# Top-k attention: a weight picked by a mark instead of a second exp; self-attention: six score banks throughout, and whole rounds of one kind

## The reference

```python
def _topk_cross_attn(h, ctx, w_q, b_q, w_kv, b_kv, w_co, b_co):
    q = (h @ w_q + b_q).reshape(B, L, H, D)
    kv = (ctx @ w_kv + b_kv).reshape(B, Lc, 2, H, D)
    scores = jnp.einsum('bqhd,bkhd->bhqk', q, k) / jnp.sqrt(jnp.float32(D))
    top_s, top_i = jax.lax.top_k(scores, TOPK)          # TOPK = 16
    attn = jax.nn.softmax(top_s, axis=-1)
    o = jnp.einsum('bhqk,bhqkd->bqhd', attn, vg).reshape(B, L, C)
    return o @ w_co + b_co

def mha(x, ctx, ...):                                   # third attention: ctx = x
    scores = jnp.einsum('bqhd,bkhd->bhqk', q, k) / np.sqrt(HD)
    attn = jax.nn.softmax(scores.astype(jnp.float32), axis=-1)
    out = jnp.einsum('bhqk,bkhd->bqhd', attn, v).reshape(Bq, Nq, D)
    return out @ wo + bo
```

## Time and profile before

| what | value |
|---|---|
| median of 3 runs | 1722.9 us (1711.07 to 1726.58) |
| the profiled execution | 1712.03 us, of which the span is 1710.2 us |
| busy: PE, DVE, ACT, POOL | 86%, 54%, 45%, 15% of the span |
| first attention | up to about 211 us |
| second attention (L919 first and last) | about 210 to 648 us |
| third attention (L857 and L895) | about 650 to 1401 us |
| fourth attention and the last MLP | to the end |

### The profile page before, as it was taken

One profiled execution on the slowest core, in us unless ns is written; L12 is line 12 of the kernel. 1 busy time (PEld: TensorE's weight loads), 2 busy tenths in 40 slices (PEclk: granted clock), 3 DMA queues, 4 the chain that ended last, 5 costly groups with the idle time before them and its releaser, 6 DMA issues.

```text
span 1710.2 us, 25890 instructions
## 1 busy us (share of the span) xinstructions
PE 1475.9 (86%) x9132; PEld 749.7 (44%) x9132; DVE 915.8 (54%) x2815; ACT 768.8 (45%) x1626; POOL 258.0 (15%) x504
## 2 busy tenths in 40 slices
PE   5999857788877787998898889998889789998998
PEld 3567534454644543353243333332323135453665
DVE  2555467766878785644445556665556225451111
ACT  2254445656666561224434445554445553334221
POOL 0020053443443532000000010000100001010110
PEclk9899967679898896999999989999999998999999
DMA  5022100000000001000010000000000000000000
GB/s 168 1 81 77 48 1 13 7 1 2 4 1 2 26 1 33 1 1 1 1 62 1 0 1 1 1 1 1 1 11 1 1 2 2 11 2 4 13 16 25
DMA packets 22096, 26.78 MB, mean 16 GB/s; under 512 B 4204, under 2 KB 19634, under 8 KB 21708
## 3 DMA queue, kind: packets, MB, share of 16 engines
q1 hardware_dynamic: 21059, 25.03, 4.6%
q10 hardware_dynamic: 909, 0.10, 0.0%
HBM read 21.58 MB, written 3.08 MB: 14 GB/s over the span
## 4 chain that ended last, share of the span: by engine, by line
PE 73%; ACT 9%; DVE 8%; issue 6%; POOL 3%; DMA 0%; ACTq 0%; SPq 0%; POOLq 0%; DVEq 0%
PE bank L857 27%; PE bank L814 9%; PE bank L895 7%; PE bank L829 6%; PE bank L793 5%; PE bank L772 3%; PE bank L919 3%; ACT pr L1081 2%; ACT exp_all L1098 2%; PE bank L751 2%; DVE part_max L1294 1%; ACT h_t L1023 1%; POOL probs L1402 1%; ACT left L1104 1%; PE bank L933 1%
## 5 line engine op out<-in xcount | busy, mean ns | idle before, releaser
L1081 ACT ACTIVATE pr<-bank 128x512 f32<-128x512 f32 x656 | 355.8, 596 | 458.6 <-PE bank L857 458.1
L1294 DVE TENSOR_REDUCE part_max<-bank 128x1 f32<-128x512 f32 x512 | 328.8, 685 | 283.6 <-PE bank L857 282.6
L857 PE MATMUL bank<-slot 32*128 32x512 f32 (+1 forms) x3072 | 430.8, 532 | 18.8 <-ACT pr L1081 14.1
L857 PEld LDWEIGHTS bank<-slot 32*128 32x128 f32 x3072 | 173.8, 188 | 243.4 <-issue 161.0
L1344 POOL TENSOR_SCALAR var_eps<-mean_var 128x4 f32<-128x4 f32 x24 | 5.5, 227 | 1103.9 <-DVE mean_var L1258 1103.7
L895 PE MATMUL bank<-pr,v 128*17 128x512 f32 x1024 | 138.6, 614 | 14.3 <-ACT pr L1081 14.3
L814 PE MATMUL bank<-h_t,w_m 128*128 128x512 f32 x256 | 133.2, 646 | 6.4 <-ACT h_t L1023 4.4
L1098 ACT ACTIVATE exp_all<-bank,neg 128x154 f32<-128x154 f32 x256 | 86.2, 395 | 57.8 <-POOL neg L1389 57.1
L1319 DVE MAX8 top<-bank 128x8 f32<-128x154 f32 x256 | 69.4, 312 | 65.7 <-PE bank L919 64.4
L919 PE MATMUL bank<-kc,slot 32*128 32x154 f32 x512 | 59.9, 357 | 45.1 <-ACT exp_all L1098 44.9
L1104 ACT ACTIVATE left<-left,neg 128x154 f32<-128x154 f32 x256 | 95.4, 434 | 0.0
(11 more groups left out here) (141 smaller groups left out, 1927.6 us busy)
## 6 DMA issues: line engine op xcount, KB each, us to landing
w_m<-in_L_xcond_w_m SPq DMA_DIRECT2D x1, 2048.0 KB, 8.6
w_m<-in_L_xcond_w_m SPq DMA_DIRECT2D x2, 1024.0 KB, 6.8
w<-in_L_xcond_w SPq DMA_DIRECT2D x2, 1024.0 KB, 6.6
w_ada<-in_L_xcond_w_ada SPq DMA_DIRECT2D x1, 1792.0 KB, 10.3
x_sb<-in_x SPq DMA_DIRECT2D x6, 256.0 KB, 6.6
res_row<-rows_dram SPq DMA_DIRECT2D x12, 128.0 KB, 3.4
out_x<-x_sb SPq DMA_DIRECT2D x6, 256.0 KB, 2.1
wa<-in_L_xcond_w_qkv SPq DMA_DIRECT2D x1, 768.0 KB, 7.3
```

Source lines behind the costliest of these rows:

```text
L857: last = nc.tensor.matmul(g.bank(*tile)[:, into], left, right, start=True, stop=True)
L1081: nc.scalar.activation(m.pr[:, u % NPR, :], g.bank("s", gi, i)[:, :], ACT.Exp).then_inc(g.free("s", gi, i), 1)
L1294: nc.vector.tensor_reduce(m.part_max[:, slot, h * TB + i // 8, i // 4 % 2:i // 4 % 2 + 1], bank[:, :], axis=AX.X, op=ALU.max).then_inc(don ...
```

## The change

In the second attention `c_exp_left` is gone. In place of `c_diff` stands `c_pick` on POOL: it first turns `left2` into marks (1 where the value is exactly -1e30, else 0; one operation on 128x308), waits for that, and multiplies the marks with `exp_all`, in the same two pieces. It waits for `left2` of DVE and `c_exp_all` of ACT. `c_neg` now waits for an older `c_exp_all` instead of an older `c_exp_left`. The planned places of the steps around it move too: the turn, the copy and the product with the values come earlier, and the scores of the next token tile a little later, behind the turn and the copy.

In the third attention, scores use banks 1 to 6 for all groups, and the ring banks 0 to 2 for all. Where a round would be of one kind (m alone at the start, s alone at the end), it holds four tiles, every second time; this holds for the first attention too.

```diff
     if kind in ("m", "m_turn", "s"):
-        return (1, 2, 3, 4, 5, 6) if 20 <= step[1] < 24 else (3, 4, 5, 6)
+        return (1, 2, 3, 4, 5, 6) if attention(step[1]) == 3 else (3, 4, 5, 6)
...
     if kind == "o_turn":
-        return (0, 1) if attention(step[1]) == 2 else (0,) if 19 <= step[1] < 24 else (0, 1, 2)
+        return (0, 1) if attention(step[1]) == 2 else (0, 1, 2)
...
     s, b = step[1:3]
-    return (0, 1) if (s, b) in ((2, 1), (3, 0), (4, 0)) else (0,) if (s, b) == (5, 0) else (0, 1, 2)
+    return (0, 1) if (s, b) in ((2, 1), (3, 0), (4, 0)) else (0, 1, 2)
...
         maxima = [("m", gi_m, i) for i in (2 * xm, 2 * xm + 1)] if gm < 8 else []
+        if a != 4 and gs < 0 and c < rounds - lead:
+            maxima = [("m", gi_m, i) for i in range(2 * xm, 2 * xm + 4)] if xm % 2 == 0 else []
+        if a != 4 and gm > 7:
+            weighed = [("s", gi_s, i) for i in range(2 * xs, 2 * xs + 4)] if xs % 2 == 0 else []
...
-                    plan.at(start + (v - 1.15) * step, ("c_score", gi, t, 0), ("c_score", gi, t, 1), ("c_scores", gi, t))
+                    plan.at(start + (v - 1.1) * step, ("c_score", gi, t, 0), ("c_score", gi, t, 1), ("c_scores", gi, t))
...
-                        plan.at(t0 + 0.45 * step, ("c_exp_all", gi, t, hf))
-                        plan.at(t0 + 1.0 * step, ("c_exp_left", gi, t, hf), ("c_diff", gi, t, hf))
+                        plan.at(t0 + 0.5 * step, ("c_exp_all", gi, t, hf))
+                        plan.at(t0 + 1.0 * step, ("c_pick", gi, t, hf))
...
-                    plan.at(t1 + 0.9 * step, ("c_tail", gi, t), ("c_turn", gi, t))
-                    plan.at(t1 + 1.3 * step, ("c_copy", gi, t))
-                    plan.at(t1 + 1.8 * step, ("c_pv", gi, t))
+                    plan.at(t1 + 0.55 * step, ("c_tail", gi, t), ("c_turn", gi, t))
+                    plan.at(t1 + 0.85 * step, ("c_copy", gi, t))
+                    plan.at(t1 + 1.25 * step, ("c_pv", gi, t))
...
-        elif kind == "c_exp_left":
-            v = plan.order[step]
-            for hh in range(2):
-                act.wait_ge(m.left2_done, 2 * v + hh + 1)
-                last = nc.scalar.activation(m.left2[:, v % 4, hh, :], m.left2[:, v % 4, hh, :], ACT.Exp, bias=m.neg2[:, v % 4, hh:hh + 1])
-            last.then_inc(m.left_exp, 1)
...
-            since(pool, (m.left_exp, v - 3))
+            since(pool, (m.all_done, v - 3))
...
-            pool.wait_ge(m.left_exp, v + 1)
+            pool.wait_ge(m.left2_done, 2 * v + 2)
+            pool.wait_ge(m.all_done, v + 1)
...
-            nc.gpsimd.tensor_tensor(m.tails[:, u % 2, hh, 0:TAIL], m.exp_all[:, v % 4, :, P:S2], m.left2[:, v % 4, :, P:S2], ALU.subtract)
-            nc.gpsimd.tensor_tensor(m.probs[:, u % 2, hh, :], m.exp_all[:, v % 4, :, 0:P], m.left2[:, v % 4, :, 0:P],
-                                    ALU.subtract).then_inc(m.diff_done, 1)
+            left, weights = m.left2[:, v % 4, :, :], m.exp_all[:, v % 4, :, :]
+            nc.gpsimd.tensor_scalar(left, left, -FAR, None, ALU.is_equal).then_inc(m.marked, 1)
+            pool.wait_ge(m.marked, v + 1)
+            nc.gpsimd.tensor_tensor(m.tails[:, u % 2, hh, 0:TAIL], left[:, :, P:S2], weights[:, :, P:S2], ALU.mult)
+            nc.gpsimd.tensor_tensor(m.probs[:, u % 2, hh, :], left[:, :, 0:P], weights[:, :, 0:P], ALU.mult).then_inc(m.pick_done, 1)
```

More of the change, by code:

```diff
@@ L266, in group_run @@
         maxima = [("m", gi_m, i) for i in (2 * xm, 2 * xm + 1)] if gm < 8 else []
+        if a != 4 and gs < 0 and c < rounds - lead:
+            maxima = [("m", gi_m, i) for i in range(2 * xm, 2 * xm + 4)] if xm % 2 == 0 else []
+        if a != 4 and gm > 7:
+            weighed = [("s", gi_s, i) for i in range(2 * xs, 2 * xs + 4)] if xs % 2 == 0 else []
         tiles = [x for both in zip(weighed, maxima) for x in both] if len(weighed) == len(maxima) else maxima + weighed
-        plan.at(t, *tiles, ("scores", *tiles))
+        if tiles:
+            plan.at(t, *tiles, ("scores", *tiles))
         plan.at(t + 0.3 * width, *[("m_red",) + x[1:] for x in maxima], *[("exp",) + x[1:] for x in weighed])
@@ L295, in topk_run @@
                         plan.at(t0, ("c_top", gi, t, hf), ("c_neg", gi, t, hf))
-                        plan.at(t0 + 0.45 * step, ("c_exp_all", gi, t, hf))
-                        plan.at(t0 + 1.0 * step, ("c_exp_left", gi, t, hf), ("c_diff", gi, t, hf))
+                        plan.at(t0 + 0.5 * step, ("c_exp_all", gi, t, hf))
+                        plan.at(t0 + 1.0 * step, ("c_pick", gi, t, hf))
                         v += 1
                     t1 = start + v * step
-                    plan.at(t1 + 0.9 * step, ("c_tail", gi, t), ("c_turn", gi, t))
-                    plan.at(t1 + 1.3 * step, ("c_copy", gi, t))
-                    plan.at(t1 + 1.8 * step, ("c_pv", gi, t))
+                    plan.at(t1 + 0.55 * step, ("c_tail", gi, t), ("c_turn", gi, t))
+                    plan.at(t1 + 0.85 * step, ("c_copy", gi, t))
+                    plan.at(t1 + 1.25 * step, ("c_pv", gi, t))
                     if t % 4 == 3:
-                        plan.at(t1 + 2.3 * step, ("o_copy", gi, half))
-                        plan.at(t1 + 2.7 * step, ("o_turn", gi, half))
-                        plan.at(t1 + 3.2 * step, ("o_norm", gi, half))
+                        plan.at(t1 + 1.6 * step, ("o_copy", gi, half))
+                        plan.at(t1 + 2.0 * step, ("o_turn", gi, half))
+                        plan.at(t1 + 2.4 * step, ("o_norm", gi, half))
     return start + 128 * step
@@ L514, in memory @@
     m.picked, m.left1_done, m.left2_done = sem("picked"), sem("left1_done"), sem("left2_done")
-    m.silu_c_done, m.silu_done, m.o_copied, m.all_done, m.left_exp = (
-        sem(n) for n in ("silu_c_done", "silu_done", "o_copied", "all_done", "left_exp"))
-    m.ident_done, m.consts, m.var_done, m.rstd_done, m.row_added, m.out_gated, m.m2_gated, m.neg_done, m.diff_done, m.mask_set = (
-        sem(n) for n in ("ident_done", "consts", "var_done", "rstd_done", "row_added", "out_gated", "m2_gated", "neg_done", "diff_done", "mask_set"))
+    m.silu_c_done, m.silu_done, m.o_copied, m.all_done = (
+        sem(n) for n in ("silu_c_done", "silu_done", "o_copied", "all_done"))
+    m.ident_done, m.consts, m.var_done, m.rstd_done, m.row_added, m.out_gated, m.m2_gated, m.neg_done, m.pick_done, m.mask_set, m.marked = (
+        sem(n) for n in ("ident_done", "consts", "var_done", "rstd_done", "row_added", "out_gated", "m2_gated", "neg_done", "pick_done", "mask_set", "marked"))
     return m
@@ L925, in tensor_program @@
             u = plan.n("c_copy", gi, t)
-            pe.wait_ge(m.diff_done, 2 * u + 2)
+            pe.wait_ge(m.pick_done, 2 * u + 2)
             nc.tensor.transpose(bank[:, 0:P], m.tails[:, u % 2, :, :].rearrange("p h e -> p (h e)"), m.ident[:, :]).then_inc(m.turned, 1)
@@ L1094, in scalar_program @@
                 act.wait_ge(*g.group_end(7))
-            since(act, (m.diff_done, v - 3))
+            since(act, (m.pick_done, v - 3))
             bank = g.bank("c_score", *step[1:])
@@ L1325, in vector_program @@
                 nc.vector.max(m.top[:, v % 2, hh, 8:16], m.left1[:, v % 2, hh, :]).then_inc(m.picked, 1)
-            since(dve, (m.diff_done, v - 3))
+            since(dve, (m.pick_done, v - 3))
             for hh in range(2):
```

2 lines of the change are left out of this document (1 added, 1 removed).

## The result

| | before | after |
|---|---|---|
| median | 1720.96 us (1711.07 to 1726.58) | 1694.62 us (1693.09 to 1701.44, 4 runs) |
| ratio to before | | 0.9875, 95% interval 0.9843 to 0.9907 |
| span of the profiled execution, mean granted clock | 1710.2 us, 0.924 | 1691.3 us, 0.921 |

The change gains 1.25%, some 21 us by the ratio, where 82 were forecast; the median lies above the forecast of 1638 and above the stated range, which ended at 1690. The page's first part, beside the earlier trace rows, shows what moved: ACT lost 75 us of work, POOL gained 128.

What follows compares the result with a forecast made beforehand. PE was taken as the bound (busy 86%), except a serial chain in the second attention's quiet part. Gains 40 + 7.5 + 14 + 5 + 16 = 82 us from 1712.03 gave 1630, median 1638, case range 1610 to 1668, stated range 1592 to 1690.

Steps and rivals of the forecast that it cites:

- change 2: Third attention's banks and whole rounds (first attention's rounds too): terms of 7.5, 14, 5, 16 and 0 us gained.
- Change 1: Second attention: dropping two ACT instructions a half for one POOL operation shortens the chain, gaining 40 us.
- The second attention does nothing: Rival: POOL's loop no faster than the old one, mark over 1.4 us, total around 1700; chance 0.04.
- E: Time of the added POOL mark over 308 columns, second attention: taken as 0.50 us, bounded 0.43 to 0.84.
- dear mark: Rival: the mark costs a two-input operation or more; second attention's change gives 22 us or less, total 1658; chance 0.17.
- (a): Third attention's start, group 16: m tiles alone stand in 16 PE pieces instead of 23, gaining 7.5 us.
- Shared banks bite: Rival: third attention's scores and ring steps wait for each other's banks, 110 us lost, total 1750; chance 0.08.
- (b): Third attention's mixed rounds with six banks instead of four: 14 us gained, between 6 and 20.
- (c): Third attention, groups 20 to 23: ring steps and projections no longer wait for bank 0 alone; 5 us, 0 to 10.
- (d): Third attention's end, s tiles alone: four exps in 2.25 us instead of 3.15, gaining 16 us, between 10 and 18.
- (e): First attention: three rounds made whole at each end; 0 us, between -2 and 3.
- The clock: Rival: denser PE work in the second attention's quiet part is granted 2.4 GHz, total 1618, down to 1600; chance 0.15.

Runs made afterwards that it cites:

- E2: Kernel before with only the third attention's change (banks and whole rounds), second attention as before; 1687.6 us, ratio 0.9823 to before.
- E1: Kernel before with only the second attention's change (mark for second exp, new planned places); 1724.5 us, ratio 1.0046 to before.
- E8: Changed kernel with eight operation forms taking turns in the mark's place, executed once for durations; the mark's form 0.98 to 1.0 us, total time not compared.
- E3: Changed kernel without the mark and its wait, POOL multiplying `left2` itself with `exp_all`; 1657.3 us, ratio 0.9646 to before.
- E12: Changed kernel with the mark made for one head of two (154 of 308 columns); 1676.4 us, ratio 0.9744 to before.
- E4: Changed kernel with `c_pick` planned at 1.04 of a step, so the next negation precedes it on POOL; 1700.3 us, ratio 0.9895 to before.
- E11: Changed kernel without the mark and with the next negation ahead of each pick on POOL; 1662.6 us, ratio 0.9677 to before.
- E6: Changed kernel without mark, negation first, scores ahead of turn, ACT's copy behind half B's exp, products with values later; 1650.1 us, ratio 0.9597 to before.
- E5: Changed kernel, mark kept, with the second attention's planned places of before; 1707.2 us, ratio 0.9928 to before.
- E9: Kernel before with whole rounds of one kind alone (first and third attention), old banks; 1696.8 us, ratio 0.9882 to before.
- E10: Kernel before with the third attention's bank change alone, old rounds; 1702.9 us, ratio 0.9909 to before.
- E7: E2 with `c_diff` planned at 1.04 of a step, so the negation precedes the subtraction; second exp kept; 1655.9 us, ratio 0.9634 to before.

## Why the prediction was wrong

**The direction was right, the third attention in the main, the second attention was not.** Of 82 us, change 2 had 42.5 and measured 30 (E2). Change 1 had 40 and measured -8 (E1). The miss is 12 and 48. The nearest of the stated outcomes is the rival "The second attention does nothing", around 1700 with a chance of 0.04, and it stands on a mark of over 1.4 us; of the signs of being wrong, "E over 0.9" came true, and in group 16 PE waiting on `hidden` at L863 (1.6 us, and 5.1 at L820).

**The step that failed: "It reads one stream and writes one, so I take 0.50, near the lower end."** E measured 0.985 (E8: 0.990), outside both bounds. The upper bound took it for granted that an operation with one input can't cost more than one with two; L1421 against L1405 in E8 says it can, 0.70 against 0.99, and so does the prediction's own 0.84 for two different tensors. The rival "dear mark" had the right cause, but stopped at 0.84 and so at 22 us of gain. With 0.985 the prediction's own loop gives 2 x (2.03 + 0.985) = 6.03 us a token tile, and 6.53 with its 0.5 for PE: that is near the means measured, 6.36 without the long opening spacing and 6.72 with it, and would have cut the 22 us for the quiet spacings to 17 x 0.32 = 5. The Trainium skill (GPSIMD Engine Reference, section 4.1 Engine selection), whose rule of one-input operations at roughly line-rate was weighed there, is not borne out by this operation: the estimate from that page's 1.03 cycles an element was 0.26 us, and E8 has 0.98 to 1.0 (only the copy, 0.455, comes near).

**A second error lies under it.** E3 has no mark at all, and gains 30 us over E2, which has the second attention of before (0.9646 against 0.9823): less than the 40 that were forecast with a mark of 0.50. E12 has a mark of 0.60, where the prediction's sum gives about 34 us: 17 x (6.85 - 5.26 - 0.5) = 18.5 for the quiet spacings, and 16 for the rest. Against E2, E12 gained 14 us by the ratios, and its second attention is 10 us shorter (434.3 for 444.4). So some 20 us would have been missing with a correct E. "PE leaves it as well: the turn and scores fill the time in which POOL and ACT pass the halves to each other" was wrong: PE has the turn ahead of the scores, the turn waits for POOL's pick, and DVE for the scores (the timeline after; E4, E11). That place is worth at most the 12 to 14 us from E11 to E6, given an early negation; E6 also moved ACT's copy and the products with the values, so its share is not shown by itself. What holds E6 at 5.68 us instead of DVE's 4.1 was not tried; in its windows DVE is busy 16.2 of 20 us at one place and PE has a clock of 0.57 at another, so one cause for all of it is not likely.

**Of the other terms of change 1**, the 13 us for the long spacings can't be told apart from the rest. The 63 spacings of before add up to 426 us, not 436; no term hangs on that. The gain of the new places (9 to 12, E5) is part of what the prediction counted, and real.

**(a) 7.5 us for whole m rounds: about 6.8 by themselves** (E1 to E9, at one clock), and -0.9 in the changed kernel. The step "in a stretch where PE has hardly a gap" held while the banks were apart. What the sum put at nothing is the wait for shared banks: PE's idle time in group 16 rose from 7.2 to 16.5 us. That is the rival "Shared banks bite" in small: it stood at 110 us, and some 5 to 8 are what shows. **(b) and (c), 14 + 5 us for banks: 18.7** in the mixed rounds (E10), 13.7 from before to after. The sum is about right, its parts are not. From the L1303 of group 16 to that of group 19, where (b) said 14, E10 gained 8.1 us. From there to group 23, where (c) said 5, it gained 10.6, nearly all of it in group 22, where the ring had bank 0 alone: 91.3 us became 81.6. **(d) 16: 13.6**, with four exps every 2.17 us, where 2.25 was said. **(e)** 0, and the start came 2.4 us earlier. The rest of the program, from the third attention's last product on, took 305 to 314 us, and it goes with the clock granted there: 313.0 to 313.7 us at 0.96, 309.8 to 310.4 at 0.97, and 304.5 to 305.4 at 0.99.

**The clock did not come up to full**: 0.68 for 0.57 in the quiet window, 0.921 for 0.924 in the mean. In the fastest kernels the mean rose a little, to 0.935 (E6 and E7).

## What to carry to other kernels

When a step in a loop is replaced by one that the trace doesn't hold, the bound from "similar" rows is only as good as the class they are put in: measure the new instruction by itself at its size first, since it is multiplied by every turn. Write the loop out in full, with what stands ahead of each of its members on every in-order queue; the engine that "leaves the chain" may sit in a second loop just behind it. Compare short stretches of two profiles only beside a third with the same instructions there, and look at the granted clock of each (E1 in group 16). And before taking a step away, try the order of the queue around it: one planned place (E7) gave more than the whole change.

## What the runs showed of the hardware

On GpSimd an operation of a tensor with a number, float32, took 0.60 us for 154 columns and 0.98 to 1.0 for 308, whatever the operation (equal, greater or equal, minimum, multiply), so about 2.5 ns a column; with two operations 1.26 (E8). A product of one tensor with itself took 0.70, a copy 0.455. The form with a number is thus the dearest of the three, by 40% and by a factor of two. For two different tensors the rows of before give an estimate of 0.84.

The same list of instructions, group 16 alone with PE busy over nine tenths of the time, took 80.1 us at a granted clock of 0.88 (before) and 85.3 at 0.82 (E1).
